# Channel attention of layer 3: the scores made a second time, turned, with the maximum added on TensorE

## The chip, the cores and the metric

One Trainium2 chip, one of its cores. The metric is the device time in microseconds (us) of the whole program, eight stages (four layers, each an attention and a feed-forward part) of which the change touches one. Lower is better.

## The reference, cut to what matters

The stage adds a channel attention to x. Of each of the 16 batches, 128 rows of 256 channels, x is normalised, and q, k and v all have the shape 128 x 256. The 128 rows are 8 heads of 16; attention runs between channels, so that the scores of a head are 256 x 256.

```python
x = x + _L3_xattn_ref(_layernorm(x, axis=-1), ctx_2048, ctx_2048)
qh = q.reshape(b * h, d // h, m)          # h = 8 heads of 16 rows, m = 256 channels
kh = k.reshape(b * h, d // h, -1)
vh = v.reshape(b * h, c // h, -1)
qk = jnp.einsum('bdm,bdn->bmn', qh, kh) * scale
ret = jnp.einsum('bmn,bcn->bcm', jax.nn.softmax(qk, axis=-1), vh)
```

## The kernel before

The stage is `channel_attention` (lines 938 to 1287). Five engines run programs of their own and meet at semaphores. There is no planner: the order of work on each engine is the order in which its `batch` function is written, and `over_tiles` runs that function for 16 batches (2 unrolled, a loop of 6 times 2, 2 unrolled).

Of each batch two halves (c = 0, 1) hold four heads each (j = 0 to 3); the rows of an odd or even head are the other 16 of a strip of 32, and are zeroed in `q_head`, so a head's scores are matmuls with 32 contraction rows. The way of one head:

- TensorE makes the scores in two matmuls of 128 queries by 256 keys (`scores`, L1210) into one of four banks `ps_s`. The four heads of a half lie in different strips of 32 rows.
- VectorE finds the negated maximum of each query (`find_max`, L1074), a query being a partition.
- ScalarE takes the exponential with that maximum as its per-partition bias, in two instructions of 256 (`exps`, L1160), into `prob`.
- TensorE turns the 256 x 256 probabilities in four 128 x 128 transposes (`turn_prob`, L1222) into `ps_t`, because the product with v needs the keys on the partitions; ScalarE copies the even heads out (`copy_probT`, L1168), VectorE the odd ones (L1081).
- TensorE multiplies with v (`weigh_values`, L1235), in which a column of ones gives the sum of the exponentials. Four heads lie in four strips of 32 columns. ScalarE copies `ps_o` (`copy_o`, L1174), TensorE turns it (`turn_o`, L1242), VectorE divides by the sum (`weigh`, L1086 and L1091), TensorE turns the result (`turn_attn`, L1250), and VectorE adds it to x (`add_to_x`, L1096).

GpSimd meanwhile adds the results of the preceding expert stage to x (`gather`, `combine`), and makes the inverse deviation, xn and `q_head` of each batch (`find_rstd` L1026, `spread` L1037 and L1041); it is ahead of TensorE by about a batch. SyncE loads `ctx` and `ctxT` two batches ahead, and at the end the experts of the next stage. On TensorE the batch function is: scores of half 0; `turn_o` and `turn_prob` of earlier batches around `weigh_values`; `turn_attn`; scores of half 1; then the same again for half 0 of this batch.

Of the kernel before, what the change touches and what calls it, by code (L numbers as in the profile page):

```python
# [936 lines left out]

def channel_attention(core, name):
# [4 lines left out]
    with core.stage() as st:  # L943
# [21 lines left out]
        ps_s = [core.ps(f"{name}_ps_s{s}", [P, W4], F32, st) for s in range(4)]
        ps_t = [core.ps(f"{name}_ps_t{s}", [P, W4], F32, st) for s in range(2)]
        ps_o = core.ps(f"{name}_ps_o", [P, D], F32, st)
        ps_out = core.ps(f"{name}_ps_out", [P, D], F32, st)
        (const_done, combined, var_done, q_spread, v_done, s_put, max_done, exp_done, t_put, t_done_v, t_done_a, pv_put, o_done,
         r_put, attn_done, a_put, x_done) = (sem(n) for n in (  # L970
             "const_done", "combined", "var_done", "q_spread", "v_done", "s_put", "max_done", "exp_done", "t_put",
             "t_done_v", "t_done_a", "pv_put", "o_done", "r_put", "attn_done", "a_put", "x_done"))
        ctx_in = [sem(f"ctx_in{u}") for u in range(2)]
        block = st.enter_context(nc.Block())

        def ctx_loaded(eng, b, u):
            eng.wait_ge(ctx_in[u], (b - u) * 16 + 32)

        @block.sync
        def _(sp):  # L980
# [1995 lines left out]
```

## Time and profile before

| | us |
|---|---|
| Median of 3 runs | 1596.16 (1592.63 to 1598.41) |
| Span of the profiled execution, first to last instruction | 1562.7 |
| Median less span (start and end of the program) | 33.5 |
| Stage: first scores to last instruction of the stage | 1199.98 to 1384.65 |

Busy over the whole span: PE 1345.7 us (86%), DVE 1023.1 (65%), ACT 829.3 (53%), POOL 627.0 (40%). The profiled execution's own time is its span and what lies around it; the page gives the span alone, so the difference of the second and third row is carried over unchanged. Times below are us from the first instruction. PE is TensorE's matmuls, PEld its weight loads, DVE VectorE, ACT ScalarE, POOL GpSimd. A 32-bit matmul shows as two records, a 32-bit transpose as one. A busy matmul record is not the time that it takes from the next: matmuls overlap, and the distance between the starts of blocks counts.

### The profile page before, as it was taken

The page shows a single profiled execution, that of the slowest core. Times are in us where ns is not written, and L with a number is a line of the kernel's source. Part 1 is how long each engine was busy: PE and PEld are TensorE (multiplying, and loading weights), DVE is VectorE, ACT ScalarE, POOL GpSimd, SP SyncE. Part 2 cuts the span into 40 slices and gives each one's busy share as a digit, 9 for nine tenths or more (in the row PEclk, how much of TensorE's full clock was granted, in tenths as well). Part 3 has the DMA queues.
Part 4 walks back from the last instruction along what each step waited for, and adds up shares of the span by engine and source line. Part 5 has one row for each costly group of instructions (what it writes and reads, how often), then busy time and mean ns, then how long its engine had stood idle before and what let it go on. Part 6 is the DMA issues. An engine that isn't in the chain of part 4 may idle for free. (4 is left out here: it accounts for less than half of the span.)

```text
span 1562.7 us, 29997 instructions
## 1 busy us (share of the span) xinstructions
PE 1345.7 (86%) x8381; PEld 881.4 (56%) x8382; DVE 1023.1 (65%) x2409; ACT 829.3 (53%) x2371; POOL 627.0 (40%) x660
## 2 busy tenths in 40 slices
PE   5899996798689888899989999978996999978993
PEld 3555553466444353576555666554773666656992
DVE  5898897477469847333655888875334888864224
ACT  3767764687420045331107888843442888835561
POOL 3112420899477232673001111112545665214661
PEclk9999998899799878999997999998996999997997
DMA  5131000500000061695301000241552111411225
GB/s 188 48 100 36 17 16 28 191 0 1 27 27 0 1 193 42 186 308 181 94 14 31 24 23 23 69 147 41 146 143 81 49 54 30 176 58 58 87 87 168
DMA packets 96448, 124.82 MB, mean 80 GB/s; under 512 B 11117, under 2 KB 76464, under 8 KB 96112
## 3 DMA queue, kind: packets, MB, share of 16 engines
q1 hardware_dynamic: 85760, 95.80, 19.4%
q0 software_dynamic: 10608, 28.07, 6.3%
q8 instruction: 37, 0.61, 0.2%
q14 instruction: 43, 0.35, 0.1%
HBM read 91.31 MB, written 33.43 MB: 80 GB/s over the span
## 5 line engine op out<-in xcount | busy, mean ns | idle before, releaser
L717 ACT ACTIVATE l0a_prob<-l0a_ps_s,l0a_neg_max 128x128 f32<-128x128 f32 x512 | 137.9, 398 | 73.2 <-DVE l0a_neg_max L559 67.6
L717 ACT ACTIVATE l2a_prob<-l2a_ps_s,l2a_neg_max 128x128 f32<-128x128 f32 x512 | 138.7, 402 | 26.0 <-DVE l2a_neg_max L559 21.3
L1160 ACT ACTIVATE l3a_prob<-l3a_ps_s,l3a_neg_max 128x256 f32<-128x256 f32 x256 | 104.5, 483 | 31.9 <-DVE l3a_neg_max L1074 30.4
L219 POOL TENSOR_TENSOR ln_rstd<-ln_var_eps,minus_half 128x4 f32<-128x4 f32 (+1 forms) x14 | 23.0, 1651 | 244.6 <-POOLq L183 213.4
L559 DVE TENSOR_REDUCE l2a_neg_max<-l2a_ps_s 128x4 f32<-128x512 f32 x128 | 85.7, 684 | 20.2 <-PE l2a_ps_s L815 19.3
L502 POOL TENSOR_TENSOR l2a_k_head<-l2a_kT,head_of_row 128x512 f32<-128x512 f32 x32 | 33.1, 1054 | 157.5 <-DMA l2a_kT<-k_rows 157.5
L568 DVE COPY l0a_probT<-l0a_ps_t 128x512 f32<-128x512 f32 x128 | 84.7, 683 | 14.9 <-PE l0a_ps_t L827 14.8
L559 DVE TENSOR_REDUCE l0a_neg_max<-l0a_ps_s 128x4 f32<-128x512 f32 x128 | 85.5, 684 | 10.2 <-PE l0a_ps_s L815 9.6
L1074 DVE TENSOR_REDUCE l3a_neg_max<-l3a_ps_s 128x2 f32<-128x512 f32 x128 | 84.0, 680 | 10.7 <-PE l3a_ps_s L1210 10.5
L1832 PE MATMUL l1a_ps_y<-l1a_kv,l1a_tap 128*128 128x512 f32 x192 | 85.6, 609 | 3.7 <-POOL l1a_kv L1804 3.7
L502 POOL TENSOR_TENSOR l0a_k_head<-l0a_kT,head_of_row 128x512 f32<-128x512 f32 x32 | 32.6, 1039 | 139.8 <-DMA l0a_kT<-k_rows 139.8
L827 PE MATMUL l2a_ps_t<-ident,l2a_prob 128*128 128x128 f32 x512 | 76.3, 283 | 7.7 <-DVE l2a_probT L568 6.9
L827 PEld LDWEIGHTS l2a_ps_t<-ident,l2a_prob 128*128 128x128 f32 x512 | 57.1, 143 | 42.2 <-DVE l2a_probT L568 24.7
L2772 PE MATMUL l3f_ps_g<-l3f_xinT,l3f_w_now 128*128 128x128 f32 x624 | 76.0, 275 | 0.0
L827 PE MATMUL l0a_ps_t<-ident,l0a_prob 128*128 128x128 f32 x512 | 70.5, 275 | 4.4 <-DVE l0a_probT L568 4.4
L2772 PEld LDWEIGHTS l3f_ps_g<-l3f_xinT,l3f_w_now 128*128 128x128 f32 x624 | 72.8, 192 | 0.1
L2428 DVE TENSOR_TENSOR l3f_hT_sb<-l3f_ps_g,l3f_act_sb 128x256 f32<-128x256 f32 x39 | 16.6, 425 | 85.6 <-PE l3f_ps_l L2799 78.0
L1222 PE MATMUL l3a_ps_t<-ident,l3a_prob 128*128 128x128 f32 x512 | 70.0, 281 | 1.2 <-ACT l3a_probT L1168 1.0
L1804 POOL TENSOR_TENSOR l1a_kv<-l1a_vT,ctxT_all 128x1024 f32 (+1 forms) x32 | 61.6, 1947 | 20.1 <-PE l1a_ps_y L1832 19.7
L805 PE MATMUL l0a_ps_s<-l0a_mask,identb 128*128 128x512 bf16 x128 | 49.7, 393 | 22.7 <-ACT l0a_prob L717 22.7
L568 DVE COPY l2a_probT<-l2a_ps_t 128x512 f32<-128x512 f32 x96 | 64.8, 682 | 5.1 <-PE l2a_ps_t L827 5.0
L1222 PEld LDWEIGHTS l3a_ps_t<-ident,l3a_prob 128*128 128x128 f32 x512 | 57.5, 143 | 16.5 <-ACT l3a_probT L1168 10.9
(489 smaller groups left out, 3534.2 us busy)
## 6 DMA issues: line engine op xcount, KB each, us to landing
expert_results<-zeros SPq DMA_DIRECT2D x1, 8320.0 KB, 26.3
l1f_got<-expert_results SPq DMA_DIRECT2D x16, 512.0 KB, 3.9
expert_results<-l2f_y_sb SPq DMA_DIRECT2D x47, 128.0 KB, 1.8
l1f_w_gu<-in_l1f_w_gu SPq DMA_DIRECT2D x16, 352.0 KB, 6.2
l2f_w_gu_all<-in_l2f_w_gu SPq DMA_DIRECT2D x1, 4096.0 KB, 14.0
l3f_w_gu_all<-in_l3f_w_gu SPq DMA_DIRECT2D x1, 4096.0 KB, 13.6
l3f_got<-expert_results SPq DMA_DIRECT2D x16, 256.0 KB, 5.3
l1f_w_d<-in_l1f_w_d SPq DMA_DIRECT2D x16, 176.0 KB
```

Source lines behind the costliest of these rows:

```text
L502: pool.tensor_tensor(k_head[u][:, c, :, :], kT[u][:, c:c + 1, :].broadcast_to([P, R, P]), core.head_of_row[:, :].unsqueeze(2).broadcast_to ...
L559: dve.tensor_reduce(neg_max[:, j, :], ps_s[j][:, :].rearrange("p (r k) -> p r k", r=R), AX.X, ALU.max, negate=True).then_inc(max_done, 1)
L568: dve.tensor_copy(probT[4 * c + j][:, :], ps_t[j % 2][:, :]).then_inc(t_done_v, 1)
L717: last = act.activation(prob[4 * c + j][:, r * P:r * P + P], ps_s[j][:, r * P:r * P + P], ACT.Exp, bias=neg_max[:, j, r:r + 1])
L805: pe.matmul(ps_s[j][:, :].rearrange("p (r k) -> p r k", r=R), core.identb[:, :], mask[u][:, :].unsqueeze(1).broadcast_to([P, R, P]), start ...
L827: last = pe.transpose(ps_t[j % 2][:, r * P:r * P + P], prob[4 * c + j][:, r * P:r * P + P], core.ident[:, :])
L1074: dve.tensor_reduce(neg_max[:, j, :], ps_s[j][:, :].rearrange("p (r k) -> p r k", r=2), AX.X, ALU.max, negate=True).then_inc(max_done, 1)
L1160: last = act.activation(prob[4 * c + j][:, m * D:m * D + D], ps_s[j][:, m * D:m * D + D], ACT.Exp, bias=neg_max[:, j, m:m + 1])
L1222: last = pe.transpose(ps_t[j % 2][:, k * D + m * P:k * D + m * P + P], prob[4 * c + j][:, m * D + k * P:m * D + k * P + P], core.ident[:, :])
L1804: pool.tensor_tensor(kv[u][:, c, :].rearrange("p (b j i) -> p b j i", b=B, i=N8), i_rows, j_rows, ALU.mult).then_inc(kv_done, 1)
L1832: last = pe.matmul(ps[u][c][:, cols], tap[u][:, (c - m) * P:(c - m) * P + P], kv[u][:, m, cols], start=(m == 0), stop=(m == c))
L2772: last = pe.matmul(ps_g[r % 2][:, n * P:n * P + P], w_now[r % 2][:, at:at + FCH], xinT[r % 2][:, c, :], start=(c == 0), stop=(c == KC - 1))
```

## The change

The probabilities are no longer turned. After the maximum is found, the scores are made a second time with the operands exchanged (`score_again`: keys on the partitions, queries along the free axis), and the exponential of them lands as `weigh_values` needs it. The maximum now belongs to the free axis, so it can't be ScalarE's bias. VectorE splits each negated maximum into three bf16 parts (the upper halves of the 32-bit words `word[0]`, `word[1] = word[0] - top[0]`, `word[2] = word[1] - top[1]`), TensorE turns these (`turn_shift`, two bf16 transposes a half), ScalarE copies them to `shiftT` (`copy_shift`), and a bf16 matmul with ones as weights (`take_shift`, 32 rows, 512 columns) adds them in the bank where `score_again` accumulates. `exps` is one instruction of 512 elements without a bias.

A batch now passes through three iterations in place of about two: first scores, maximum and split; then the second scores, the exponential and the product with v of half 0; then the product of half 1 and the result. Buffers of a batch come in threes, `prob` stays in eight, `probT` is gone; PSUM holds three banks of first scores, three of second scores, and two of `ps_o` which also take `ps_turn` and `ps_out`. `over_threes` runs 3 iterations unrolled, a loop of 3 times 3, and iterations 12 to 17 unrolled. SyncE's loads are unrolled, three batches ahead.

```diff
+def over_threes(eng, body):
+    for b in range(3):
+        body(b, b, 0)
+    with eng.Fori(1, 4) as i:
+        for r in range(3):
+            body(i * 3 + r, r, i)
+    for b in range(12, B + 2):
+        body(b, b % 3, b // 3)
 ...
+        PAIRS = ((0, 1), (2, 3))
+        LATER = (2, 3, 0, 1)
 ...
+            for b in range(3, B):
+                sp.wait_ge(e_put, (b - 2) * CH)
+                sp.wait_ge(v_done, b - 2)
+                load_ctx(b, b % 3)
 ...
         def _(pool):
-            for u in range(2):
-                pool.memset(v_aug[u][:, :, :, :], 0.0).then_inc(const_done, 1)
+            pool.memset(onesb[:, :], 1.0).then_inc(const_done, 1)
+            for c in range(2):
+                pool.memset(shifts[c][:, :], 0.0).then_inc(const_done, 1)
+            for r in range(3):
+                pool.memset(v_aug[r][:, :, :, :], 0.0).then_inc(const_done, 1)
 ...
         def _(dve):
-            def copy_probT(b, c, j):
-                dve.wait_ge(t_put, b * CH + 4 * c + j + 1)
-                ...
-                dve.tensor_copy(probT[4 * c + j][:, :], ps_t[j % 2][:, :]).then_inc(t_done_v, 1)
+            def split(c, b=None):
+                word, top = shift_word[c], shift_top[c]
+                dve.drain()
+                if b is not None:
+                    row_stats(dve, core, b)
+                dve.tensor_tensor(word[:, :, :, 1], word[:, :, :, 0], top[:, :, :, 0], ALU.subtract)
+                dve.drain()
+                dve.tensor_tensor(word[:, :, :, 2], word[:, :, :, 1], top[:, :, :, 1], ALU.subtract).then_inc(split_done, 1)
 ...
         def _(act):
-                for m in range(2):
-                    last = act.activation(prob[4 * c + j][:, m * D:m * D + D], ps_s[j][:, m * D:m * D + D], ACT.Exp,
-                                          bias=neg_max[:, j, m:m + 1])
+            def exps(b, r, c, at):
+                n = b * CH + 4 * c + at
+                act.wait_ge(e_put, n + 1)
+                if at == 0 and after(b, 1):
+                    act.wait_ge(pv_put, b * 2 + c - 1)
+                act.activation(prob[4 * c + LATER[at]][:, :], ps_e[(r * CH + 4 * c + at) % 3][:, :], ACT.Exp).then_inc(exp_done, 1)
+            def copy_shift(b, c):
+                act.wait_ge(turn_put, b * 2 + c + 1)
+                act.activation(shiftT[c][:, :], ps_turn[1 - c], ACT.Copy).then_inc(turn_done, 1)
 ...
+            def batch(b, r, turn):
+                weighed = within(b, 1, B + 1)
+                if weighed:
+                    exps(b - 1, (r - 1) % 3, 0, 0)
+                    exps(b - 1, (r - 1) % 3, 0, 1)
+                if within(b, 2, B + 2):
+                    copy_o(b - 2, 1)
+                if weighed:
+                    exps(b - 1, (r - 1) % 3, 0, 2)
+                    exps(b - 1, (r - 1) % 3, 0, 3)
+                    copy_shift(b - 1, 1)
+                    exps(b - 1, (r - 1) % 3, 1, 0)
+                    exps(b - 1, (r - 1) % 3, 1, 1)
+                    copy_o(b - 1, 0)
+                    exps(b - 1, (r - 1) % 3, 1, 2)
+                    exps(b - 1, (r - 1) % 3, 1, 3)
+                if within(b, 0, B - 1):
+                    values(b + 1, (r + 1) % 3, turn + (r == 2))
+                if within(b, 0, B):
+                    copy_shift(b, 0)
 ...
+            def take_shift(b, r, c, at):
+                n, j = b * CH + 4 * c + at, LATER[at]
+                rows = slice(32 * j, 32 * j + 32)
+                if at == 0:
+                    pe.wait_ge(turn_done, b * 2 + c + 1)
+                if c or at == 3 or after(b, 1):
+                    pe.wait_ge(exp_done, n - 2)
+                pe.matmul(ps_e[(r * CH + 4 * c + at) % 3][:, :].rearrange("p (t m) -> p t m", t=2), onesb[rows, :],
+                          shiftT[c][rows, :].unsqueeze(1).broadcast_to([32, 2, D]), start=True, stop=False)
+            def score_again(b, r, c, at, t):
+                j = LATER[at]
+                rows = slice(32 * j, 32 * j + 32)
+                mm = pe.matmul(ps_e[(r * CH + 4 * c + at) % 3][:, t * D:t * D + D], ctx[r][rows, t * P:t * P + P],
+                               q_head[r][rows, c, :], start=False, stop=(t == 1))
+                if t:
+                    mm.then_inc(e_put, 1)
 ...
+            def scores(b, r, turn, s):
+                c, first, ats = s // 2, PAIRS[s % 2], PAIRS[s % 2]
+                new, old = within(b, 0, B), within(b, 1, B + 1)
+                if new and s == 0:
+                    pe.wait_ge(ctx_in[r], turn * 32 + 32)
                     pe.wait_ge(q_spread, b + 1)
+                before = (b - 1, (r - 1) % 3, c)
+                if new:
+                    for j in first:
+                        score(b, r, c, j, 0)
+                if old:
+                    for at in ats:
+                        take_shift(*before, at)
+                    for at in ats:
+                        score_again(*before, at, 0)
+                if new:
+                    for j in first:
+                        score(b, r, c, j, 1)
+                if old:
+                    for at in ats:
+                        score_again(*before, at, 1)
 ...
+            def batch(b, r, turn):
+                old, done = within(b, 1, B + 1), within(b, 2, B + 2)
+                r1, r2 = (r - 1) % 3, (r - 2) % 3
+                scores(b, r, turn, 0)
+                if done:
+                    weigh_values(b - 2, r2, 1)
+                scores(b, r, turn, 1)
+                if old:
+                    turn_shift(b - 1, 1)
+                if done:
                     turn_o(b - 2, 1)
+                scores(b, r, turn, 2)
+                if old:
+                    weigh_values(b - 1, r1, 0)
+                if done:
+                    turn_attn(b - 2, r2)
+                scores(b, r, turn, 3)
+                if old:
                     turn_o(b - 1, 0)
+                if within(b, 0, B):
+                    turn_shift(b, 0)
```

VectorE's batch is `weigh(b-2, 0)`, two `find_max`, `look_at`, two `find_max`, `split(0)`, `weigh(b-2, 1)`, `find_max`, `keep_stats`, `find_max`, `add_to_x(b-2)`, two `find_max`, `split(1)` with the row statistics of b-2.

## Rows read from the trace of the kernel before

**Rows 1.** Windows: start:end, length, busy us of each engine (records), granted clock, DMA
```profile
1200.00:1222.00 22.00, 19.38 (x139) 13.83 (x140) 13.67 (x25) 14.13 (x37) 15.40 (x20) 0.68 0.26 73
1288.00:1310.00 22.00, 20.57 (x215) 15.01 (x211) 19.38 (x45) 18.67 (x48) 11.71 (x19) 1.00 0.13 36
```
**Rows 2.** Waits of the stage, 1200 to 1390: total us, times, longest
```profile
ACT l3a_prob L1160 <- DVE l3a_neg_max L1074: 30.4, 33, 4.2
PEld l3a_ps_t L1222 <- ACT l3a_probT L1168: 10.9, 24, 0.5
```
**Rows 3.** Groups by line and shape, 1190 to 1395: busy us, mean ns, idle before
```profile
L1160 ACT ACTIVATE l3a_prob<-l3a_ps_s,l3a_neg_max 128x256 f32<-128x256 f32 x256 | 104.5, 483 | 31.9 <-DVE l3a_neg_max L1074 30.4
L1074 DVE TENSOR_REDUCE l3a_neg_max<-l3a_ps_s 128x2 f32<-128x512 f32 x128 | 84.0, 680 | 10.7 <-PE l3a_ps_s L1210 10.5
L1222 PE MATMUL l3a_ps_t<-ident,l3a_prob 128*128 128x128 f32 x512 | 70.0, 281 | 1.2 <-ACT l3a_probT L1168 1.0
L1081 DVE COPY l3a_probT<-l3a_ps_t 128x512 f32<-128x512 f32 x64 | 43.9, 687 | 18.4 <-PE l3a_ps_t L1222 18.4
L1168 ACT ACTIVATE l3a_probT<-l3a_ps_t 128x512 f32<-128x512 f32 x64 | 38.8, 607 | 2.1 <-PE l3a_ps_t L1222 2.1
```
**Rows 4.** Timeline, one batch: start us, length, engine, work, idle before
```profile
1281.59 0.25 PEld L1250 LDWEIGHTS l3a_ps_out<-ident,l3a_attn 128*128 128x128 f32 x2
1282.00 1.14 PEld L1210 LDWEIGHTS l3a_ps_s<-l3a_ctx,l3a_q_head 32*128 32x128 f32 x16 [0.17 <-issue]
1282.01 1.54 PE L1210 MATMUL l3a_ps_s<-l3a_ctx,l3a_q_head 32*128 32x256 f32 x16
1282.25 0.60 ACT L1168 ACTIVATE l3a_probT<-l3a_ps_t 128x512 f32<-128x512 f32 x1
1282.73 0.40 ACT L1174 ACTIVATE l3a_o_sb<-l3a_ps_o 128x256 f32<-128x256 f32 x1
1283.47 0.20 PEld L1242 LDWEIGHTS l3a_ps_o<-ident,l3a_o_sb 128*128 128x128 f32 x2 [0.33 <-ACT l3a_o_sb L1174]
...
1287.43 1.27 PEld L1210 LDWEIGHTS l3a_ps_s<-l3a_ctx,l3a_q_head 32*128 32x128 f32 x16 [0.17 <-issue]
1287.43 1.68 PE L1210 MATMUL l3a_ps_s<-l3a_ctx,l3a_q_head 32*128 32x256 f32 x16
...
1288.39 0.57 POOL L1026 TENSOR_TENSOR ln_rstd<-ln_mean_var,minus_half 128x1 f32<-128x1 f32 x1 [1.86 <-DVE ln_mean_var L1069]
1289.04 0.20 PEld L1242 LDWEIGHTS l3a_ps_o<-ident,l3a_o_sb 128*128 128x128 f32 x2 [0.33 <-ACT l3a_o_sb L1174]
...
1290.42 1.07 PE L1235 MATMUL l3a_ps_o<-l3a_probT,l3a_v_aug 128*32 128x256 f32 x16
```
**Rows 5.** Timeline, start of the stage
```profile
1194.88 0.99 POOL L999 MEMSET l3a_v_aug<- 128x512 f32 x2 [6.23 <-POOLq L183]
...
1196.11 0.89 POOL L1026 TENSOR_TENSOR ln_rstd<-ln_var_eps,minus_half 128x3 f32<-128x3 f32 x1
...
1199.98 2.11 PE L1210 MATMUL l3a_ps_s<-l3a_ctx,l3a_q_head 32*128 32x256 f32 x16 [9.96 <-POOL l3a_q_head L1041]
...
1211.80 2.38 PE L1210 MATMUL l3a_ps_s<-l3a_ctx,l3a_q_head 32*128 32x256 f32 x16
```
**Rows 6.** Timeline, end of the stage; the first row is batch 15
```profile
1362.41 1.68 PE L1210 MATMUL l3a_ps_s<-l3a_ctx,l3a_q_head 32*128 32x256 f32 x16
...
1377.05 0.59 PEld L1235 LDWEIGHTS l3a_ps_o<-l3a_probT,l3a_v_aug 128*32 128x32 f32 x16 [0.17 <-issue]
...
1378.05 0.20 PEld L1250 LDWEIGHTS l3a_ps_out<-ident,l3a_attn 128*128 128x128 f32 x2 [0.41 <-issue]
...
1380.08 1.07 PE L1235 MATMUL l3a_ps_o<-l3a_probT,l3a_v_aug 128*32 128x256 f32 x16 [1.02 <-DVE l3a_attn L1091]
...
1384.50 0.15 DVE L214 TENSOR_SCALAR ln_var_eps<-ln_mean_var 128x1 f32<-128x1 f32 x1
```
**Rows 7.** Groups by line and shape of other stages, whole span
```profile
L2639 ACT ACTIVATE l1f_s_act<-l1f_ps_g 128x512 f32<-128x512 f32 x10 | 6.0, 597 | 58.5 <-PE l1f_ps_u L2669 58.5
L1832 PE MATMUL l1a_ps_y<-l1a_kv,l1a_tap 128*128 128x512 f32 x192 | 85.6, 609 | 3.7 <-POOL l1a_kv L1804 3.7
```

More of the change, by code:

```diff
@@ L965, in channel_attention @@
[L965 to L972, printed above, removed]
@@ L1173, in copy_o @@
                     act.wait_ge(r_put, b * 2 + c - 1)
-                act.activation(o_sb[c][:, :], ps_o[:, :], ACT.Copy).then_inc(o_done, 1)
-            def batch(b, u):
-                for c in range(2):
-                    before = (b, 0) if c else (b - 1, 1)
-                    exps(b, c, 0)
-                    exps(b, c, 1)
-                    if c or after(b, 1):
-                        copy_probT(*before, 0)
-                    exps(b, c, 2)
-                    exps(b, c, 3)
-                    if c or after(b, 1):
-                        copy_probT(*before, 2)
-                    if after(b, 1):
-                        copy_o(b - 1, c)
-                    if c == 1 and ahead(b, 1):
-                        values(b + 1, 1 - u)
@@ L1192, in _ @@
[L1192 to L1198 removed]
+                act.activation(o_sb[c][:, :], ps_o[c][:, 0:D], ACT.Copy).then_inc(o_done, 1)
+            def batch(b, r, turn):
[18 more added lines that the diff above has]
+                    copy_shift(b, 0)
@@ L1200, in _ @@
+            act.wait_ge(const_done, 11)
+            values(0, 0, 0)
+            over_threes(act, batch)
         @block.tensor
         def _(pe):
-            def scores(b, c, u):
-                if c == 0:
-                    ctx_loaded(pe, b, u)
-                    pe.wait_ge(q_spread, b + 1)
-                for m, j in ((0, 0), (0, 1), (0, 2), (1, 0), (1, 1), (1, 2), (0, 3), (1, 3)):
-                    rows = slice(32 * j, 32 * j + 32)
-                    if m == 0 and (c or after(b, 1)):
-                        pe.wait_ge(exp_done, b * CH + 4 * c + j - 3)
-                    mm = pe.matmul(ps_s[j][:, m * D:m * D + D], q_head[u][rows, c, m * P:m * P + P], ctx[u][rows, :],
-                                   start=True, stop=True)
-                    if m:
-                        mm.then_inc(s_put, 1)
@@ L1226, in weigh_values, with score @@
-            def weigh_values(b, c, u):
-                pe.wait_ge(t_done_a, b * 4 + 2 * c + 2)
-                pe.wait_ge(t_done_v, b * 4 + 2 * c + 2)
+            def score(b, r, c, j, m):
+                n = b * CH + 4 * c + j
+                rows = slice(32 * j, 32 * j + 32)
+                if m == 0 and (c or j == 3 or after(b, 1)):
+                    pe.wait_ge(max_done, n - 2)
+                mm = pe.matmul(ps_m[(r * CH + 4 * c + j) % 3][:, m * D:m * D + D], q_head[r][rows, c, m * P:m * P + P],
+                               ctx[r][rows, :], start=True, stop=True)
+                if m:
+                    mm.then_inc(s_put, 1)
@@ new lines, in turn_shift @@
+            def turn_shift(b, c):
+                pe.wait_ge(split_done, b * 2 + c + 1)
+                if c == 0 and after(b, 2):
+                    pe.wait_ge(x_done, b - 1)
+                if c and after(b, 1):
+                    pe.wait_ge(attn_done, b * 2 - 1)
+                for m in range(2):
+                    last = pe.transpose(ps_turn[1 - c][:, m * P:m * P + P],
+                                        shift_top[c][:, m, :, :].rearrange("p j w -> p (j w)"), core.identb[:, :])
+                last.then_inc(turn_put, 1)
@@ L1287 @@
+            over_threes(pe, batch)
 MAGIC = 1.5 * 2.0 ** 23
```

252 lines of the change are left out of this document (104 added, 148 removed).

## The prediction

> **What bounds the kernel now.** I read first the windows over the stage. In mid-stage TensorE is busy 20.57 of 22 us, VectorE 19.38, ScalarE 18.67, at the full granted clock (1.00, 2.4 GHz); in the first 22 us the clock is 0.68 [rows 1]. Then the period: the scores of batch 1 start at 1211.80 and those of batch 15 at 1362.41 [rows 5, 6], so a batch takes 150.61 / 14 = 10.76 us. Then the waits: ScalarE waits on VectorE's maximum 30.4 us, and the transposes on the copies of the probabilities 10.9 us in waits of at most 0.5 [rows 2]. So the three engines hold each other closely, TensorE ahead. Last the timeline, for what one block costs the next. GpSimd is no bound: it waits 1.86 us a batch for VectorE [rows 4], so its own work is 10.76 - 1.86 = 8.9 us.
>
> **Removed, per batch.** 32 transposes: 70.0 / 16 = 4.4 us of TensorE. Eight copies of 512: 43.9 / 16 = 2.7 us of VectorE and 38.8 / 16 = 2.4 us of ScalarE. Sixteen exponentials of 256, 104.5 / 16 = 6.5 us, become eight of 512 [rows 3].
>
> **Price of the new pieces.**
> - Exponential of 512 without a bias: none in the trace. The nearest is another function of 512 from PSUM without bias, 597 ns [rows 7], like the copy of 512, 607 ns [rows 3]. After that copy the next instruction starts 0.48 us later (1282.25 to 1282.73), an overlap of 0.12 [rows 4]. I take 0.60 long, 0.48 apart. Above, two exponentials of 256 less their overlaps are 0.72 apart; below, 0.45.
> - `copy_shift`: 256 elements, like `copy_o`, 0.40 [rows 4]. `values`, also 256, costs 0.40 - 0.12 = 0.28 before the next.
> - One pass of 256 columns of 32 bits: 85.6 / 192 / 2 = 0.22 us [rows 7]. A block of scores holds eight 32-row matmuls in four strips that overlap: 1.54 and 1.68 us to its last end, and 1.47 and 1.61 to the next block's first load (1282.00 to 1283.47, 1287.43 to 1289.04) [rows 4]. Four passes lie behind each other in a strip, and the fourth strip, issued last, begins about two later, so I read six.
> - A new quarter is five deep: in the strip of a second score, `take_shift` (one bf16 pass of 512 columns, taken as 0.22; bounds 0.1 and 0.44) and four passes of `score_again`; the first scores run in the other two strips beside it. So a quarter takes 1.61 - 0.22 = 1.39 to its end (1.61 being the mean of 1.54 and 1.68) and 1.54 - 0.22 = 1.32 to the next block; I take 1.39 and 1.30. Bounds: 1.29 and 1.25 if `take_shift` is nearly free; the whole old block, 1.66 and 1.60, if first scores get in its way.
> - Product with v: 1.00 to the next block (1377.05 to 1378.05) [rows 6]; above, 1.07 [rows 4]. `turn_attn`: 0.41 (1281.59 to 1282.00) [rows 4], I take 0.40. `turn_shift`: two bf16 transposes, between nothing and `turn_o`'s 0.44; 0.25.
> - VectorE: `split` is two tiny operations of about 0.15 (as the last row of [rows 6]) with two drains, between 0.3 and 1.0 a half. Its batch is 19.38 / 22 x 10.76 = 9.5 less 2.7 plus 0.6 to 2.0: 7.4 to 8.8. It stays under the period found below; its splits are done some 4 us before TensorE turns them, which is what covers them. Without that cover each us of lateness would be a us of the chain.
>
> **Sums by engine mislead.** TensorE: four quarters 5.2, two products 2.0, `turn_attn` 0.4, two `turn_o` and two `turn_shift` 1.05: 8.7 us. ScalarE: 8 x 0.48 + 4 x 0.3 + 0.3 = 5.3. That looks like a gain of 1.9 us a batch. But the order adds a wait: `take_shift` waits for `copy_shift`, which stands behind the four exponentials of the half before in ScalarE's queue, and these need TensorE's preceding quarter. Behind the waiting `take_shift` stand the quarter's `score_again`, the product, the next quarter, and so the next exponentials. Laid end to end from one `copy_shift` to the next, with 0.05 for each hand-over (an estimate: the copy of `o_sb` that starts at 1282.73 ends 0.34 before the load that it releases, so no row here is a clean one; bounds 0.03 and 0.3):
>
> First half: hand-over 0.05, quarter 0 to next block 1.30, product 1.00, quarter 1 to its end 1.39, hand-over 0.05, two exponentials 0.96, `copy_shift` 0.40. Sum 5.15.
> Second half: the same 5.15, with `turn_attn` 0.40 between product and quarter 3, and `values` 0.28 ahead of the copy. Sum 5.83.
> Period 10.98 against 10.76: +0.22 us a batch. `turn_o`, `turn_shift` and two first scores lie beside the exponentials; TensorE idles some 2 us a batch, ScalarE about half.
>
> Low end with every bound low: 2 x (0.03 + 1.25 + 1.00 + 1.29 + 0.03 + 0.90 + 0.38) + 0.35 + 0.25 = 10.4. High end with the upper values of quarter and exponential: 2 x (0.05 + 1.60 + 1.07 + 1.66 + 0.05 + 1.44 + 0.40) + 0.41 + 0.40 = 13.4; these don't come together, since most have a near row. I keep 10.6 to 11.7.
>
> **The edges.**
> - Start: 1194.88 to 1196.11 is GpSimd's setup, 1.23 us for two buffers of 128 x 512 at 0.5 each and small ones [rows 5]. Added are one such buffer (0.5), two half as large (0.5) and three small (0.3): +1.3, all on the path, since TensorE waits 9.96 us for `q_head`. First scores at 1201.3.
> - Iteration 0 has first scores alone. Before, it lasted 1199.98 to 1211.80 = 11.8 us at half clock. After, four quarters of first scores at 2.1 each (the first old block at half clock took 2.11 [rows 5]) end at 1209.5; transposes and copy, about 0.85: the first `take_shift` goes at 1210.35.
> - Iteration 1 lacks one product and `turn_attn`: 10.98 - 1.4 = 9.6. The clock: 0.68 over 22 us is 14 us at half [rows 1], so it rises at 1214. I leave it there: some 3.7 us of iteration 1 at 1.2 GHz lose half of that, 1.8. Iteration 2 begins at 1221.7.
> - 14 iterations (2 to 15) of 10.98: 1375.4.
> - Iteration 16 makes second scores only; its chain is as long, less `values` and `copy_shift`, plus the last exponential's tail: 10.4, to 1385.8. Then hand-over and the last product at 1385.85. Before, it started at 1380.08 and the stage ended 4.57 later, at 1384.65 [rows 6]; the same chain follows: 1390.4.
>
> So the stage ends 5.8 us later; nothing behind it changes. The expert load goes out when 13 batches' second scores are done; before, it went with the first scores of the fourteenth, about the same iteration, and is used long after.
> Profiled: 1562.7 + 5.8 = 1568.5; with the 33.5 that lie around the span, 1602.0. One tenth of a us in the period is worth 1.6 us (iterations 1 to 16).
>
> A second score loads 128 columns of weights for 32 rows, as an old score does: 16 loads in 1.14 and 1.27 us [rows 4], about 0.075 each, in four strips at once. The Trainium skill, "TensorE: Matmul & The Clock Gate", section "LDWEIGHTS (loading the stationary operand)", says that a load costs its columns over 1.2 and that a 32-row load takes as long as a 128-row one, which speaks against the exchange of wide transposes for thin matmuls: taken one after another, 18 loads of a quarter would be an estimated 1.92 us. The rows already go faster than that rule taken serially.
>
> **Rivals.**
> 1. Loads bind the quarter (or passes of different strips don't fully overlap). 18 loads at 0.075 are 1.35, plus the 0.33 that lay between the last load and the next block (1283.47 - 1283.14) [rows 4]: 1.68 in place of 1.30. Four quarters: +1.5 us a batch, 24 us: 1626. Partly so, half of it: 1614. For: the old blocks' loads fill nearly their length. Against: in the old block the six passes explain the same length. Chance 0.13.
> 2. Faster: the copy of the maximum leaves the path. Place: `take_shift`'s wait. It decides when ScalarE ends its two exponentials and the copy (1.41 after the quarter) before TensorE has gone through the quarter's tail, `turn_o`, `turn_shift` and the next first scores, about 0.9. If ScalarE is quicker there, or the quarters shorter, so that the wait is under 0.2, TensorE's 8.7 and GpSimd's 8.9 bind: period 9.0, 16 x 2.0 = 32 less: 1570. Halfway, 1586. For: all engine sums are under 9. Against: ScalarE works in order, and nothing lets the copy pass the exponentials. Chance 0.17.
> 3. The clock falls in mid-stage because TensorE idles about 2 us a batch. For each iteration at 1.2 GHz the passes in four quarters and two products double, about 5 us; half of the iterations: +40, 1642. Against: the clock is 1.00 with TensorE's idle of 1.4 in 22 us [rows 1], and no idle would be over 1.3 us at once. Chance 0.03.
> 4. The change does what it says but is the same in time: period 10.6 to 10.8, 1596 to 1599. This is the low part of the forecast.
>
> **Chances.** The forecast, period 10.6 to 11.4, has 0.67: 1596 to 1609, likeliest 1602. Rival 1 has 0.13, rival 2 0.17, rival 3 0.03. A measurement here tells about 0.3% (4.8 us) from no change. Slower by more: 0.37 of the forecast's part, and 0.16 of rivals 1 and 3: 0.53. Within: 0.30 of the forecast's part. Faster: 0.17, rival 2. The range reaches halfway to both sides: 1585 to 1614.
>
> **What would show it.** Right: in mid-stage a period near 11.0 between `turn_attn` blocks; TensorE's longest wait that of `take_shift` for `copy_shift`, about 0.5 to 1.2 us, twice a batch; ScalarE idle about half, waiting on the second scores; VectorE near 8 us a batch; the quarter 1.3 to the next block; an exponential of 0.6. Wrong: no wait at `take_shift` (rival 2), a quarter over 1.5 (rival 1), a granted clock under 1.00 behind the first 20 us (rival 3), or TensorE waiting on `split`.

## The result and the profile after

| | before | after |
|---|---|---|
| Median, same chip | 1595.70 us (5 runs, 1592.63 to 1598.41) | 1601.79 us (5 runs, 1600.55 to 1604.73) |
| Ratio, 95% interval | | 1.0043 [1.0028, 1.0058] |
| On another chip | 1599.42 us (24 runs) | 1602.73 us (12 runs), ratio 1.0032 [1.0011, 1.0052] |
| Span of the profiled execution | 1562.7 | 1598.5 |
| Stage, GpSimd's first memset to its last instruction | 189.8 (191.5 in a second profile) | 192.9 (193.9 in a second profile) |

The change costs 0.3 to 0.4%. The two spans must not be subtracted. After's profiled execution took 1600.55 us for a span of 1598.5, so only 2.05 us lie around a span; the first profile of before is then of an execution of some 1564.8 us, 31 us under the median and under every time in the table. Where the 31 us lie is told under the hardware. The medians count every run, but the ratios leave out a stray slow one (2825 us once in e2; 2616 and 1615 us once each in the kernel before).

Windows of the stage: the 22 us from the first scores, then mid-stage (columns as in [rows 1]).
```profile
1217.00:1239.00 22.00, 21.06 (x129) 13.70 (x129) 11.70 (x24) 6.02 (x11) 15.32 (x20) 0.55 0.17 48
1300.00:1322.00 22.00, 20.46 (x231) 12.43 (x230) 16.26 (x44) 11.84 (x26) 14.12 (x21) 1.00 0.16 48
```
In mid-stage ScalarE is down from 18.67 to 11.84 of 22 us and VectorE from 19.38 to 16.26, but TensorE is as full as before (20.57 to 20.46): fewer instructions on each engine and no gain. The first window shows what I had not seen coming: the mean clock is 0.55 (0.68 before [rows 1]), since it is at half until 26.0 us behind GpSimd's first memset, 19.8 us behind the first scores (before: 19.1 and 14.0).

Groups of the stage, 1205 to 1410: line, engine, operation, shapes, count | busy us, mean ns | idle before and what ended it. They answer to [rows 3].
```profile
L1230 PE MATMUL l3a_ps_m<-l3a_ctx,l3a_q_head 32*128 32x256 f32 x512 | 94.2, 442 | 12.5 <-POOL l3a_q_head L1064 11.4 <-DVE l3a_shifts L1099 0.8 <-issue 0.2
...
L1186 ACT ACTIVATE l3a_prob<-l3a_ps_e 128x512 f32<-128x512 f32 x128 | 69.7, 595 | 75.8 <-PE l3a_ps_e L1248 75.7
L1248 PE MATMUL l3a_ps_e<-l3a_q_head,l3a_ctx 32*128 32x256 f32 x512 | 69.3, 386 | 0.0
L1230 PEld LDWEIGHTS l3a_ps_m<-l3a_ctx,l3a_q_head 32*128 32x128 f32 x512 | 52.5, 198 | 28.8 <-issue 19.3 <-DVE l3a_shifts L1099 7.4
L1248 PEld LDWEIGHTS l3a_ps_e<-l3a_q_head,l3a_ctx 32*128 32x128 f32 x512 | 51.2, 193 | 1.9
...
L1190 ACT ACTIVATE l3a_shiftT<-l3a_ps_o 128x256 bf16<-128x256 bf16 x32 | 12.4, 388 | 12.6 <-issue 12.2 <-PE l3a_ps_o L1282 0.3
```
The exponentials fell from 104.5 us [rows 3] to 69.7, as priced (595 ns each, 0.60 forecast). But ScalarE now sits idle 75.7 us ahead of them, waiting for the second scores: the time saved became waiting.

Waits of 1230 to 1400: total us, times, longest. They answer to [rows 2].
```profile
ACT l3a_prob L1186 <- PE l3a_ps_e L1248: 74.6, 63, 2.4
DVE l3a_shifts L1099 <- PE l3a_ps_m L1230: 26.6, 41, 2.0
...
PEld l3a_ps_e L1242 <- ACT l3a_shiftT L1190: 17.6, 24, 1.3
...
PE l3a_ps_e L1242 <- ACT l3a_shiftT L1190: 9.5, 19, 1.0
```
ScalarE waits for TensorE's second scores (L1248), and TensorE for ScalarE's copy of the maximum (L1190), ahead of the matmul that adds it (L1242). Two engines that wait for each other are one chain. (PEld and PE are the same engine: the two figures overlap and are not summed.)

The timeline of one batch shows the chain link by link (start, length, engine, work, idle before; answers to [rows 4]).
```profile
1305.28 0.39 PE L1242 MATMUL l3a_ps_e<-l3a_shiftT,l3a_onesb 32*128 32x512 bf16 x2 [0.56 <-ACT l3a_shiftT L1190]
...
1305.61 0.26 POOL L1053 TENSOR_SCALAR l3a_shift<-ln_mean_var,ln_rstd 128x1 f32<-128x1 f32 x1 [1.40 <-issue]
...
1306.46 1.07 PE L1298 MATMUL l3a_ps_o<-l3a_prob,l3a_v_aug 128*32 128x256 f32 x16
1306.64 1.08 ACT L1186 ACTIVATE l3a_prob<-l3a_ps_e 128x512 f32<-128x512 f32 x2 [1.42 <-PE l3a_ps_e L1248]
...
1307.46 0.48 PE L1230 MATMUL l3a_ps_m<-l3a_ctx,l3a_q_head 32*128 32x256 f32 x2
...
1308.66 0.29 PE L1282 MATMUL l3a_ps_o<-identb,l3a_shifts 128*128 128x128 bf16 x2
1308.76 1.08 ACT L1186 ACTIVATE l3a_prob<-l3a_ps_e 128x512 f32<-128x512 f32 x2 [0.76 <-PE l3a_ps_e L1248]
...
1309.73 0.39 ACT L1190 ACTIVATE l3a_shiftT<-l3a_ps_o 128x256 bf16<-128x256 bf16 x1
...
1310.18 0.39 PE L1242 MATMUL l3a_ps_e<-l3a_shiftT,l3a_onesb 32*128 32x512 bf16 x2
...
1311.36 1.07 PE L1298 MATMUL l3a_ps_o<-l3a_prob,l3a_v_aug 128*32 128x256 f32 x16
1311.47 1.09 ACT L1186 ACTIVATE l3a_prob<-l3a_ps_e 128x512 f32<-128x512 f32 x2 [1.34 <-PE l3a_ps_e L1248]
```
First half: take of the maximum to the product 1.18 (1305.28 to 1306.46), product to next quarter 1.00, that quarter to the exponentials 1.30, two exponentials 0.97, copy to the next take 0.45: 4.90. The second half has `turn_attn` (0.37) and `values` (0.31) as well: 5.58. Period 10.47. The result of L1282, which the copy needs, is there 0.8 us before the copy starts at 1309.73: the copy is late because it stands behind two exponentials.

Start and end of the stage (answers to [rows 5, 6]):
```profile
1210.86 0.20 POOL L1018 MEMSET l3a_onesb<- 128x128 bf16 x1 [5.42 <-POOLq L183]
...
1217.12 2.08 PE L1230 MATMUL l3a_ps_m<-l3a_ctx,l3a_q_head 32*128 32x256 f32 x10 [11.40 <-POOL l3a_q_head L1064]
...
1226.93 0.61 PE L1242 MATMUL l3a_ps_e<-l3a_shiftT,l3a_onesb 32*128 32x512 bf16 x2
...
1389.30 0.39 PE L1242 MATMUL l3a_ps_e<-l3a_shiftT,l3a_onesb 32*128 32x512 bf16 x2 [0.97 <-ACT l3a_shiftT L1190]
...
1399.16 1.07 PE L1298 MATMUL l3a_ps_o<-l3a_prob,l3a_v_aug 128*32 128x256 f32 x16 [0.80 <-ACT l3a_prob L1186]
...
1403.60 0.15 DVE L214 TENSOR_SCALAR ln_var_eps<-ln_mean_var 128x1 f32<-128x1 f32 x1
```
First scores at +6.26 from the first memset (5.10 before), first take at +16.07, second take of a batch's half 0 at +29.4; the last batch's chain is 9.86 long and the tail 4.59 (4.57 before).

### The profile page after: what moved, and what is told of

It reads as the page before. It is cut to its first block and busy times, and to the rows that moved or that the text cites. A ratio compares the mean times of both kernels' runs of the same rounds, so it can differ in the third digit from the quotient of the medians.

```text
span 1598.5 us, 29769 instructions
## 1 busy us (share of the span) xinstructions
PE 1364.9 (85%) x8573; PEld 874.3 (55%) x8574; DVE 1001.3 (63%) x2409; ACT 774.4 (48%) x2211; POOL 628.2 (39%) x665
## 5 line engine op out<-in xcount | busy, mean ns | idle before, releaser
L717 ACT ACTIVATE l2a_prob<-l2a_ps_s,l2a_neg_max 128x128 f32<-128x128 f32 x512 | 138.3, 401 | 26.0 <-DVE l2a_neg_max L559 21.2
L1099 DVE TENSOR_REDUCE l3a_shifts<-l3a_ps_m 128x2 f32<-128x512 f32 x128 | 83.8, 687 | 39.4 <-PE l3a_ps_m L1230 37.6
L1186 ACT ACTIVATE l3a_prob<-l3a_ps_e 128x512 f32<-128x512 f32 x128 | 69.7, 595 | 75.8 <-PE l3a_ps_e L1248 75.7
L1230 PE MATMUL l3a_ps_m<-l3a_ctx,l3a_q_head 32*128 32x256 f32 x512 | 94.2, 442 | 12.5 <-POOL l3a_q_head L1064 11.4
L1856 POOL TENSOR_TENSOR l1a_kv<-l1a_vT,ctxT_all 128x1024 f32 (+1 forms) x32 | 61.6, 1946 | 20.1 <-PE l1a_ps_y L1884 19.8
L1248 PE MATMUL l3a_ps_e<-l3a_q_head,l3a_ctx 32*128 32x256 f32 x512 | 69.3, 386 | 0.0
L805 PE MATMUL l0a_ps_s<-l0a_mask,identb 128*128 128x512 bf16 x128 | 50.7, 402 | 21.2 <-ACT l0a_prob L717 21.0
L1230 PEld LDWEIGHTS l3a_ps_m<-l3a_ctx,l3a_q_head 32*128 32x128 f32 x512 | 52.5, 198 | 28.8 <-issue 19.3
```

What stands on the lines that cost most here:

```text
L717: last = act.activation(prob[4 * c + j][:, r * P:r * P + P], ps_s[j][:, r * P:r * P + P], ACT.Exp, bias=neg_max[:, j, r:r + 1])
L1099: dve.tensor_reduce(shift_word[c][:, :, j, 0], ps_m[(r * CH + 4 * c + j) % 3][:, :] .rearrange("p (m k) -> p m k", m=2), AX.X, ALU.max, ne ...
L1186: act.activation(prob[4 * c + LATER[at]][:, :], ps_e[(r * CH + 4 * c + at) % 3][:, :], ACT.Exp).then_inc(exp_done, 1)
L1230: mm = pe.matmul(ps_m[(r * CH + 4 * c + j) % 3][:, m * D:m * D + D], q_head[r][rows, c, m * P:m * P + P], ctx[r][rows, :], start=True, sto ...
L1248: mm = pe.matmul(ps_e[(r * CH + 4 * c + at) % 3][:, t * D:t * D + D], ctx[r][rows, t * P:t * P + P], q_head[r][rows, c, :], start=False, s ...
L1856: pool.tensor_tensor(kv[u][:, c, :].rearrange("p (b j i) -> p b j i", b=B, i=N8), i_rows, j_rows, ALU.mult).then_inc(kv_done, 1)
```

## Experiments

Each ran against the kernel before on its own chip; ratios are to that. Three groups, three chips: e0 to e3, e4 to e7, f1 to f4. "Period" is from one first-half take to the next, in the last iterations (written out in the code) unless said otherwise.

**e0: the kernel before, again**, for a profile that stands beside a normal execution.

> The kernel before, profiled once more. In the first profile of it the span is 1562.7 us, in that of the changed kernel 1598.5, 35.8 apart, while the medians differ by 6. Theory 1: the first profile caught a short execution, and the difference lies in the stages l1f and l3f, which the change doesn't touch; then this profile has a span near 1593, and its stage from GpSimd's first memset to the last VectorE instruction is again 189.8 us, against 192.9 with the change. Theory 2: the change lengthens l1f or l3f (its code is longer); then l1f and l3f are short again here. Time: ratio 1.00 to the kernel before.

1597.28 us, ratio 1.0016 [0.9996, 1.0035]. Stage 191.5, period between `turn_attn` blocks 10.75; the clock rose 21.2 us behind the first memset, against 19.1 in the first profile. So after's stage is 1.4 us longer than this one and 3.1 longer than the first. The span is 1594.1, near the 1593 of theory 1: the long sections belong to the kernel before too. But the stage, expected at 189.8 again, is 1.7 us longer, so two profiles of one kernel differ by as much as the change costs in the stage.

**e1: no wait for the copy.** `take_shift` reads a buffer of zeros, so the maximum is not subtracted; the products with v wait for the copies instead.
```diff
-                if at == 0:
-                    pe.wait_ge(turn_done, b * 2 + c + 1)
...
-                          shiftT[c][rows, :].unsqueeze(1)...
+                          no_shift[rows, :].unsqueeze(1)...
```


> take_shift reads a constant tile of zeros in place of shiftT, and no longer waits for the copy; the turned maximum and its copy are still made, and the products with v wait for the copy because they write the bank it reads. What is left out: the maximum is not subtracted. Theory A (the chain copy, quarter, product, quarter, two exponentials, copy sets the period of 10.46 us): the copy is now needed one quarter later, so the period falls to TensorE's own 8.1 to 8.5, or to GpSimd's 8.9 while it gathers; 28 to 34 us less than the change, 1568 to 1574. Theory B (TensorE's matmuls and loads set it): under 5 us less, 1597 to 1602. Theory C (VectorE's maxima and splits): no change either.

1581.85 us, ratio 0.9911 [0.9889, 0.9932]; stage 176.5, period 8.93. Against after the stage is 16.4 us shorter and the median 20 us lower (28 to 34 were expected), with the same instructions on every engine but one more memset: the wait for the copy is what binds, not any engine's sum. The size was less than expected, since inside the loop the periods were 9.7 to 10.4 for the most part, and 11.2 and 11.5 where the clock was at half for 6.8 us.

**e2: a second copy of 256 ahead of the copy of the maximum; e3: the same copy ahead of `copy_o`.**
```diff
+                act.activation(spare[c][:, :, :], core.ident[:, :]..., ACT.Copy)
                 act.wait_ge(turn_put, b * 2 + c + 1)        # e2
...
+                act.activation(spare[c][:, :, :], core.ident[:, :]..., ACT.Copy)
                 act.wait_ge(pv_put, b * 2 + c + 1)          # e3
```


> One more ScalarE copy of 256 elements right ahead of each copy of the turned maximum. Theory A: it lies in the chain whole, 0.27 to 0.39 us twice a batch, 16 batches: +8.6 to +12.5 us on the change, 1610 to 1614. Theories B and C: ScalarE idles about half, so nothing, 1602.

> The same extra copy, but ahead of the copy of ps_o, where ScalarE waits for the product anyway. Theory A: nothing (within 2 us of the change, 1602). If ScalarE's sum of work were the bound: +8 to +12, as in the other place.

e2: 1617.59 us, ratio 1.0155 [1.0121, 1.0189], period 11.07, +0.60 for two copies. That is 9.6 us in 16 batches, as expected; the time is over the 1610 to 1614 expected, and the profiled stage is 13.3 us over after's, with the clock at half until +28.6 and in two later stretches of 3.4 us. e3: 1599.92 us, ratio 1.002 [0.9987, 1.0054], period 10.47 unchanged. The same 0.8 us of ScalarE's work a batch, on the same engine: in front of `copy_shift` it lengthens the period by its whole price in the queue, in front of `copy_o` by nothing (the times alone, good to some 5 us in e3, could not say it so well). e2's timeline:
```profile
1386.30 0.42 ACT L1190 ACTIVATE l3a_spare<-ident 128x256 f32<-128x256 f32 x1
1386.61 0.39 ACT L1192 ACTIVATE l3a_shiftT<-l3a_ps_o 128x256 bf16<-128x256 bf16 x1
...
1387.05 0.39 PE L1244 MATMUL l3a_ps_e<-l3a_shiftT,l3a_onesb 32*128 32x512 bf16 x2 [0.41 <-ACT l3a_shiftT L1192]
```
A copy of 256 is 0.42 long but 0.31 before the next: 0.31 is its price in a queue.

**e4: both copies early; e5: only that of half 1.** The copy moves ahead of the second pair of exponentials, and `turn_shift` right behind the products, so that its result is there by then. In e4 the sum with x (`add_to_x`) and `turn_attn` also go later, two waits change and one is added, since the turned maximum shares PSUM with other results. The results are the same.
```diff
                     exps(b - 1, (r - 1) % 3, 0, 1)
                 if within(b, 2, B + 2):
                     copy_o(b - 2, 1)
+                if weighed:
+                    copy_shift(b - 1, 1)
                     exps(b - 1, (r - 1) % 3, 0, 2)
                     exps(b - 1, (r - 1) % 3, 0, 3)
-                    copy_shift(b - 1, 1)
...
+                if old:
+                    turn_shift(b - 1, 1)
                 scores(b, r, turn, 1)
-                if old:
-                    turn_shift(b - 1, 1)
```
(This is all of e5's edit; e4 does the same with half 0.)

> The change with both copies of the turned maximum moved ahead in ScalarE's queue, before the second pair of exponentials of a half in place of after it; TensorE turns the maxima right behind the product with v, and turn_attn goes behind the last quarter, since a bank can be used by one engine at a time. Same arithmetic, all waits kept. Theory A: two exponentials (0.97) and part of a quarter leave the chain in each half; the period falls from 10.47 to TensorE's order, which the run without the dependence put at 8.9; VectorE's splits may come a little late, so 8.9 to 9.6: 14 to 25 us less than the change, 1577 to 1588, faster than both kernels. Theory B (loads bind): no change, 1602.

> Only the copy of half 1 is moved ahead. Theory A: only that half gets shorter, by 0.97 of exponentials and up to 0.2 more, the other half stays at 5.6: period 9.3 to 9.6, 14 to 18 us less than the change, 1584 to 1588. Theory B: 1602.

e4: 1547.83 us, ratio 0.993 [0.9908, 0.9952]; stage 175.8, period 9.11 at the end of the stage but 9.8 to 10.1 in iterations 5 to 9. e5: 1552.99 us, ratio 0.9953 [0.9939, 0.9967]; stage 184.7, period 9.99. That is more than the 9.3 to 9.6 expected: the half whose copy was moved fell from 4.90 to 4.42 only, and the other stayed at 5.57, as it should. e4's timeline:
```profile
1318.42 1.09 ACT L1187 ACTIVATE l3a_prob<-l3a_ps_e 128x512 f32<-128x512 f32 x2 [0.73 <-PE l3a_ps_e L1250]
...
1319.57 0.38 ACT L1197 ACTIVATE l3a_o_sb<-l3a_ps_o 128x256 f32<-128x256 f32 x1
...
1319.67 0.39 PE L1244 MATMUL l3a_ps_e<-l3a_shiftT,l3a_onesb 32*128 32x512 bf16 x2
...
1319.85 0.38 ACT L1191 ACTIVATE l3a_shiftT<-l3a_ps_o 128x256 bf16<-128x256 bf16 x1
...
1320.95 1.08 ACT L1187 ACTIVATE l3a_prob<-l3a_ps_e 128x512 f32<-128x512 f32 x2 [0.72 <-PE l3a_ps_e L1250]
...
1321.67 0.39 PE L1244 MATMUL l3a_ps_e<-l3a_shiftT,l3a_onesb 32*128 32x512 bf16 x2
```
The copy now starts at 1319.85, in time in which ScalarE waited anyway, and its take at 1321.67 has no idle behind a copy. This is the change's arithmetic, instruction for instruction, in another order, and it is faster than the kernel before.

**e6: 14 full-height matmuls ahead of the stage; f2: these and 4 more behind each of the first three quarters of iteration 0**, both with nobody reading the results, to see whether the half clock at the start can be shortened.
```diff
+            keep_busy(pe, core, ps_e[0], 14)
             over_threes(pe, batch)
...
+                if isinstance(b, int) and b == 0:        # f2, three times
+                    keep_busy(pe, core, ps_e[0], 4)
```


> The change with 14 matmuls of 512 columns of no use put on TensorE while it waits for the first q_head. In the profile of the change the granted clock stays at 1.2 GHz for 26.0 us from the stage's start and iteration 1 takes 13.35 us. If the light iteration 0 is what keeps it low, the clock rises some 10 us earlier and iteration 1 falls to about 9.5: 4 us less, 1598. If it doesn't hold through iteration 0's gaps: nothing, 1602.

> The changed kernel with 14 full-height matmuls of 512 columns ahead of the stage and 4 behind each of the first three quarters of iteration 0, whose results nobody reads. It asks whether the 1.2 GHz clock up to some 26 us behind the stage's start belongs to the thin 32-row work of iteration 0, since 14 matmuls at the start alone did not hold it. If the thin work sets the clock: the clock stays at 2.4 GHz from about 4 us on, the first take of the maximum comes at about stage start + 13 to 15 in place of 16.1, iteration 1 takes 10.6 in place of 13.4, and the kernel is 3 to 5 us faster than f1. Rival, that the clock takes its time whatever runs: the clock still rises at about +26 and the added matmuls cost 3 to 6 us.

e6: 1563.44 us, ratio 1.0019 [1.0008, 1.003]. f2: 1601.34 us, ratio 1.0025 [1.0, 1.005], beside 1.0032 [1.0011, 1.0052] for the unaltered kernel (f1) on that chip: no difference that can be measured. Windows of e6 (as in [rows 1]):
```profile
1196.00:1200.00 4.00, 2.36 (x16) 1.20 (x14) 0.00 (x0) 0.25 (x1) 3.34 (x8) 0.98 0.08 28
1200.00:1204.00 4.00, 2.97 (x18) 1.87 (x16) 3.40 (x7) 0.00 (x0) 3.22 (x4) 0.88 0.16 47
1204.00:1208.00 4.00, 4.00 (x22) 2.63 (x24) 2.56 (x6) 1.29 (x2) 3.09 (x4) 0.50 0.37 113
1208.00:1212.00 4.00, 4.00 (x30) 3.31 (x22) 1.43 (x3) 1.46 (x3) 2.48 (x5) 0.50 0.15 41
1212.00:1216.00 4.00, 4.00 (x27) 2.38 (x28) 2.66 (x9) 1.36 (x3) 2.53 (x3) 0.50 0.21 56
1216.00:1220.00 4.00, 4.00 (x34) 2.10 (x34) 0.74 (x3) 1.47 (x3) 2.82 (x5) 0.50 0.02 9
```
The clock was at 2.4 GHz from 3.4 us behind the first memset and fell at +10.2 (1203.0), with only thin first scores on TensorE since the added matmuls, but with idle time between them too (busy 2.36 and 2.97 of 4 us). Then it stayed at 1.2 GHz until +27.3, with TensorE shown busy in all of four windows of 4 us. The first take came at +14.36 (16.07 in after), but iteration 1 took 14.7 in place of 13.35. In f2 the clock stayed at 2.4 GHz to +18.2, so the first take came at +14.27, but it fell then, in iteration 1 and behind a wait of 1.57 us, and was back only at +25.0; iteration 1 took 13.8 again. So denser work in iteration 0 kept the clock up longer, and iteration 1 then lost what iteration 0 had won: both theories of f2 miss, since the fall and the rise moved and the time did not. Whether the thinness of the work or the idle time between it lets the clock fall is not shown.

**e7: the 18 iterations written out; f3: e4 written out; f4: f3 with f2's matmuls.**
```diff
-    for b in range(3):
-        body(b, b, 0)
-    with eng.Fori(1, 4) as i:
...
-    for b in range(12, B + 2):
+    for b in range(B + 2):
```


> All 18 iterations unrolled. In the change the unrolled iterations take 10.47 us, those of the loop 10.47 to 11.3, 2.8 us over 10.47 in sum. If the loop's register arithmetic and branches are the cause, all take 10.47: 2.8 us less, 1599. If it is GpSimd's gathers, which go on in the same iterations, the excess stays: 1602. If the longer code must be fetched late, it is slower.

> The kernel with both copies of the maximum ahead of the second pair of exponentials, and its 18 iterations written out instead of a loop. If the loop's branches and fetches hold the iterations in it at 9.3 to 10.1 where the written-out ones take 9.1: the stage is 3 to 7 us shorter than with the early copies alone, ratio about 0.989 to 0.991. Rival, that the transfers of the loads or GpSimd's work set those iterations: periods stay at 9.3 to 10.1 and the ratio at 0.993.

> Early copies, written-out iterations and the full-height matmuls of f2 together. If each of the three does what its theory says they add up: 5 to 10 us less than the early copies alone, ratio 0.987 to 0.990. If the clock's rise does not move: the same as f3 or up to 4 us slower.

e7: 1561.61 us, ratio 1.0016 [0.9999, 1.0033]; from iteration 2 to 15 every period is 10.47, where after's inside the loop vary from 10.5 to 11.3. The stage is 190.3 us, against 192.9 and 193.9 for the kernel with the loop on other chips: about 3 us, which the ratios, whose intervals overlap, bear out no more than weakly. Not all of it is the loop's: e6, which keeps the loop and ran on e7's chip, has only 1.3 us over 10.47 in iterations 2 to 9, where after has 2.8. f3: 1585.18 us, ratio 0.9905 [0.9885, 0.9925]. f4: 1584.99 us, ratio 0.9934 [0.991, 0.9958]; its matmuls bring nothing here either. Against f1 on the same chip (1602.73) f3 is 17.5 us faster, and its stage 17.1 shorter (193.9 to 176.8). Whether f3 beats e4 stays open: the intervals overlap and the two ran on different chips. The ratio lies in the range of the loop theory, but its mechanism is refuted: the stage is no shorter than e4's (176.8 against 175.8), and the written-out iterations take 10.0.

f3's periods are the new fact: 9.96 to 10.04 for iterations 2 to 9, though they are written out, and 9.1 to 9.5 behind them. GpSimd's timeline in f3:
```profile
1280.51 0.59 POOL L1044 TENSOR_TENSOR ln_rstd<-ln_mean_var,minus_half 128x1 f32<-128x1 f32 x1
1282.50 0.26 POOL L1048 TENSOR_SCALAR l3a_shift<-ln_mean_var,ln_rstd 128x1 f32<-128x1 f32 x1 [1.40 <-issue]
...
1290.51 0.59 POOL L1044 TENSOR_TENSOR ln_rstd<-ln_mean_var,minus_half 128x1 f32<-128x1 f32 x1
...
1319.54 0.96 POOL L1026 DMA_INDIRECT l2f_got<-expert_results,l2f_from_slot  x1 [0.30 <-issue]
...
1327.36 0.55 POOL L1044 TENSOR_TENSOR ln_rstd<-ln_mean_var,minus_half 128x1 f32<-128x1 f32 x1
1328.08 0.27 POOL L1048 TENSOR_SCALAR l3a_shift<-ln_mean_var,ln_rstd 128x1 f32<-128x1 f32 x1 [0.17 <-issue]
```
and the same place in the kernel before, right behind the row with 1.86 us of waiting in [rows 4]:
```profile
1289.31 0.26 POOL L1030 TENSOR_SCALAR l3a_shift<-ln_mean_var,ln_rstd 128x1 f32<-128x1 f32 x1 [0.35 <-issue]
```
Where GpSimd waited 1.86 us for VectorE between its gather and this place, the pause was 0.35; where it came straight from the gather, 1.40; and once the last gather had gone (1319.54), 0.17 without any wait. So the pause belongs to the gather, and the wait had covered 1.05 us of it. GpSimd's own work is not 10.76 - 1.86 = 8.9 but 10.0 (1280.51 to 1290.51, with no wait for another engine), and that is f3's period up to about the last gather.

That this is what holds TensorE up is shown best in e4. GpSimd has `q_head` ready there 2.5, 1.6 and 1.0 us ahead of TensorE's first scores of iterations 2 to 4, and these iterations take 8.9 to 9.3; the scores of iterations 6 to 10 start 0.13 us behind it, and iterations 5 to 9 take 9.8 to 10.1. Once the gathers are over it is more than 3 us ahead again. One such place in e4:
```profile
1262.26 1.04 POOL L1064 TENSOR_TENSOR l3a_q_head<-l3a_xn,odd_head_of_row 128x512 f32<-128x512 f32 x1
...
1263.42 0.59 PE L1232 MATMUL l3a_ps_m<-l3a_ctx,l3a_q_head 32*128 32x256 f32 x2
```
In f3 `q_head` is ready some 1.4 us ahead in each of these iterations, so the link between the two equal periods is not a direct wait there, and which one it is stays open.

**f1: the changed kernel on the third chip.**

> The changed kernel unaltered, on the same chip as the three below. My theory (the copy of the maximum stands in the chain): 0.3 to 0.6% slower than the kernel before, whatever the chip's own level. Rival, that the difference belonged to the first chip: within 0.1%.

1602.73 us, ratio 1.0032 [1.0011, 1.0052]: the small loss is the kernel's, not the first chip's. Its profile has the clock at half once more in mid-stage, for 3.4 us, and the iteration in which that falls took 12.05 in place of 10.47.

## Why the prediction was right

The time (1602.0 forecast, 1601.79 measured) and the mechanism were right: the saved work left, and a wait of TensorE for the copy of the maximum took its place. e1 (that wait gone: the stage 16 us shorter than after's), e2 and e3 (0.6 and 0.0 a batch for the same extra copy, by its place) show it. That the figure came out so close is luck: terms of the sum erred both ways, the stage grew by 1.4 to 3.1 us where 5.8 were forecast, and the medians differ by 3 us more than the profiled stages do. The forecast's own sign, a period of 10.6 to 11.4, was met on the mean (10.64, which is rival 4's 10.6 to 10.8) and missed in the written-out part (10.47).

- **Period.** 10.98 forecast, 10.47 in the written-out part and 10.64 on the mean of iterations 2 to 15. The links were right in kind and large in size: quarter to the product 1.18 (1.30 forecast), quarter to the exponentials 1.30 (1.39 + 0.05), product 1.00 (1.00), two exponentials 0.97 (0.96), `turn_attn` 0.37 (0.40), `values` 0.31 (0.28), copy and hand-over 0.45 (0.40 + 0.05). The mis-sized term is the quarter: 2 x (0.12 + 0.14) = 0.52 a batch too much, and the whole error is 10.98 - 10.47 = 0.51. A quarter that waits has its first scores done beforehand (in after's timeline before 1310.18), which the reading of an old block ([rows 4]) didn't take into account; but the quarter that doesn't wait is as much too large, so this isn't the whole reason, and the rest is not shown. 14 iterations: 4.7 us too much.
- **The start.** First scores at +6.26, +1.16 (1.3 forecast). First take at +16.07 (15.5, of which 0.2 is a slip: four quarters of 2.1 from 1201.3 end at 1209.7). But the clock was left at its rise of before, +19.1, and it rose at +26.0: iteration 1 took 13.35, where 11.4 was forecast. In all 2.6 us too little. This is the step that failed: I noted that iteration 0 has first scores alone and priced its length, but took the clock's rise over unchanged. Why it comes 7 us later stays open; that iteration 0 leaves TensorE thinner work than before fits, but e6 and f2, which made that work denser, gained no time.
- **The end.** 9.86 (10.4) and 4.59 (4.57).
- **The sum.** For the stage against the first profile 5.8 + 2.6 - 4.7 - 0.5 = 3.2, and 192.9 - 189.8 = 3.1 was measured. Against e0's profile it is 1.4. The medians differ by 6.1, by the interval 4.5 to 9.3, on the first chip and by 3.3 on the third (its interval 1.8 to 8.3), where f1's stage is 2.4 over e0's. Why the first chip's runs differ by more than the profiled stages stays open; stretches at half clock, as in f1, would do it (its longest iteration is 1.6 us over the rest), and the one profile of after has none.
- **33.5 us around the span** was a wrong reading without an effect. The term stands for the difference between a short execution and a usual one.
- **Engine sums mislead:** right. ScalarE is busy 11.84 of 22, VectorE 7.7 a batch (near 8 forecast), TensorE's own order without the wait 8.93 in e1 (8.7 forecast).

The rivals: **1**, loads bind the quarter: refuted, a quarter without a wait is 1.20 to the next block (1307.46 to 1308.66), under the 1.30 forecast. **2**, the copy leaves the path: not in this kernel, whose order forbids it, as argued; e4 makes it happen by order alone, but its stage is 17 us shorter than after's in place of 32. Of the 15 us that are missing, some 5 are there because after's own period is 10.64 and not 10.98, and most of the rest because GpSimd's 8.9 is 10.0: e4's mean over iterations 2 to 15 is 9.46, not 9.0. **3**, the clock falls in mid-stage: not as a state of half the iterations, but single stretches of 3.4 us at half clock were seen in f1, f2, f4 and e3, two in e2 and one of 6.8 in e1, and none in the profiles of before, e0, after, e4 to e7 and f3.

## What to carry to other kernels

When work is taken away from several engines at once, write down the loop of waits that stays and add up its links: the period is that loop as long as no engine's own sum is larger (as GpSimd's 10.0 was in e4), and it shows where a small operation stands behind a large one in an in-order queue. Moving that operation adds no instruction and was worth 17 us here, three to five times what the change itself lost. And an engine's idle time doesn't all belong to it as slack: it can cover something that comes back when the wait goes (here 1.05 us behind a gather).

## What the runs showed of the hardware

- **The clock and a full busy share.** In e6 TensorE was shown busy in all of four windows of 4 us one after another, and the clock stayed at 1.2 GHz through them. It rose at +19.1 and +21.2 in the kernel before, at +26.0 and +26.3 in the changed one. A full busy share in the page did not tell that the clock would rise.
- **Loads of different strips.** Of the 18 weight loads of a quarter the 16 of L1230 and L1248 are 193 to 198 ns long each: 3.1 us, one after another. The quarter passed in 1.20 us.
- **Chips differ by 36 to 40 us in this kernel.** The kernel before has medians of 1595.5, 1599.4 and 1559.8 us on three chips. In the profiles the difference lies outside the changed stage, in two expert stages (l1f and l3f): 264.2 and 152.9 us long in the short profile of before, 279.1 and 169.9 in e0. e4 to e7, on the quick chip, have 263 to 264 and 153 to 155, so the short profile looks like one of the quick chip; where it was taken is not on record. Windows over a section of the first of these stages, first profile and e0:
```profile
637.40:706.80 69.40, 67.63 (x320) 48.03 (x319) 19.85 (x52) 26.89 (x81) 53.58 (x54) 1.00 0.92 287
```
```profile
635.10:716.60 81.50, 70.98 (x320) 49.41 (x318) 19.09 (x50) 25.36 (x78) 53.62 (x54) 0.98 0.79 245
```
  The same work at 287 and at 245 GB/s (last column) takes 69.40 and 81.50 us; what slows the transfers there was not tried.
- **A pause behind a gather.** GpSimd's second instruction behind an indirect DMA started 1.40 us late when GpSimd came straight from it, 0.35 when it had waited 1.86 us in between, 0.17 with no gather in front (f3 and the kernel before).
